# The whole tanh of a recurrence step, written to PSUM instead of SBUF

## The chip, the cores and the metric

One core of one Trainium2 chip runs the whole program in one launch. The metric is the device time in microseconds from the first to the last instruction's work, median of the runs shown.

## The reference

The input is x, 8 x 1024 x 256 in fp32. Four blocks are added one after another, each on a layer norm of x:

```python
x = x + attn_a(layernorm(x))      # gated linear attention, 16 heads, and an MLP 256 -> 512 -> 256
x = x + ffn(layernorm(x))         # 8 experts of 256 x 256, the top 2 of each token are mixed
x = x + attn_b(layernorm(x))      # a plain recurrence over the 1024 tokens
x = x + ffn(layernorm(x))
```

The change is in the third block. It is strictly serial in time, with a state of 16 numbers for each of the 8 batch rows:

```python
xB = einsum('bsd,dn->sbn', x, B)
def step(h, xb_t):
    h = tanh(xb_t + h @ A.T)
    return h, h
_, hs = scan(step, h0, xB)
y = einsum('sbn,nd->bsd', hs, C) @ W_out.T + b_out
```

## The kernel before

The 1024 tokens are cut into 32 rounds of TS = 32 tokens for all 8 batch rows (TOK = 256 columns, two tiles of 128 rows). A round goes through eight stages, and a software pipeline runs them skewed: in one body, stage 0 works on round n, stage 1 on round n-1, and so on to stage 7. Each engine has its own instruction list for the body, in an order written out by hand, and semaphores tie the lists together. So every engine runs its queue strictly in order, and an instruction that waits holds all behind it.

The recurrence of a round has 32 steps, spread between the other work of the bodies of stages 4 to 7. One step crosses three engines:

- TensorE, `step` and `recur` (L1113): waits for semaphore `rnn_h`, then one matmul of the constant aT with the 8 columns of hs of the step before adds to the 8 columns of this step in PSUM bank RB (bank 5, columns 0 to 255, which a matmul at L1397 has filled with x times B for all 32 steps). It signals `rnn_mm`.
- ScalarE, `state_of` (L525, L526): waits for `rnn_mm` and takes the tanh of these 8 columns twice, 48 partitions x 8: once rounded to fp32r (h_lead), once in full fp32 (h_whole). The second signals `rnn_tanh`.
- VectorE, `split_state` (L750): waits for `rnn_tanh`. One scalar_tensor_tensor multiplies h_whole by a 0/1 number per partition (`keeps_rest`, from the constants in SBUF) and subtracts h_lead, which gives the exact value split into two fp32r parts in hs. It signals `rnn_h`, for which TensorE's next step waits.

The split into parts is how fp32 accuracy is kept with fp32r matmuls; the helper `product` (L1096) does the same for all wide products, with three matmuls for each. `combine` (L781) is VectorE's scalar_tensor_tensor that adds one expert's output from PSUM, scaled per row by `coef`, to an accumulator in SBUF. `normed` on VectorE (L771) subtracts and multiplies two scalars per row. GpSimd has 128x256 and 128x512 tensor_tensors on SBUF: the expert sums (L396, L398), the attention state (L412, L422), residuals (L415, L425, L487), and small statistics (`rstd`, L368). Bank 5 is used for the recurrence alone, and its columns 256 to 511 are free.

Of the kernel before, what the change touches and what calls it, by code (L numbers as in the profile page):

```python
# [6 lines left out]
F32 = mybir.dt.float32  # L7
F32R = mybir.dt.float32r
U32 = mybir.dt.uint32
ALU = mybir.AluOpType  # L10
ACT = mybir.ActivationFunctionType
# [3 lines left out]
B, T, D = 8, 1024, 256  # L15
TS = 32
ROUNDS = T // TS
TOK = B * TS
# [13 lines left out]
NB = 3 * N  # L32
# [14 lines left out]

BANK = {"Y0": 3, "Z": 2, "QK": 6, "VG0": 2, "VG1": 0, "KT": 6, "SD": 0, "O": 4, "OG": 7, "WO": 7, "Y1": 6, "F1A": 3,
    "F1B": 6, "F2": 6, "T1": 2, "L1": 1, "G1_0": 7, "G1_1": 2, "G1_2": 3, "G1_3": 1, "G1_4": 7, "G1_5": 6, "G1_6": 0,
    "G1_7": 7, "TR": 3, "RB": 5, "RO": 4, "T2": 0, "L2": 0, "G2_0": 2, "G2_1": 1, "G2_2": 7, "G2_3": 3, "G2_4": 2, "G2_5": 1,  # L50
    "G2_6": 0, "G2_7": 6}
# [3 lines left out]
    0: [("T2", 6, 'yT2'), ("L2", 6, 'sub2'), ("G1_6", 4, ("acc1", 2 * VECTOR_GROUPS, 10)), ("VG1", 1, 'sg1'),  # L55
            ("G2_6", 6, ("acc2", 2 * VECTOR_GROUPS, 10)), ("SD", 1, 'dstate')],
    1: [("L1", 4, 'sub1'), ("G1_3", 4, ("acc1", 2 * VECTOR_GROUPS, 6)), ("G2_1", 6, ("acc2", 2 * VECTOR_GROUPS, 2)),
            ("G2_5", 6, ("acc2", 2 * VECTOR_GROUPS, 8)), ("SD", 1, 'dstate')],
    2: [("T1", 4, 'yT1'), ("G1_1", 4, ("acc1", 2 * VECTOR_GROUPS, 2)), ("Z", 1, 'zb'), ("G2_0", 6, ("scaled2", TILES, 1)),
            ("G2_4", 6, ("scaled2", TILES, 2)), ("VG0", 1, 'sg0'), ("SD", 1, 'dstate')],  # L60
    3: [("Y0", 1, 'hT'), ("G1_2", 4, ("acc1", 2 * VECTOR_GROUPS, 4)), ("F1A", 3, 'gT'),
            ("G2_3", 6, ("acc2", 2 * VECTOR_GROUPS, 6)), ("TR", 4, 'yrT'), ("SD", 1, 'dstate')],
    4: [("O", 2, 'onorm'), ("RO", 5, 'mv_m2')],
# [31 lines left out]
def build(nc, x, wts, out):  # L95
    ctx = ExitStack()
    with ctx:
        def sb(name, shape, dt=F32):
            return ctx.enter_context(nc.sbuf_tensor(name, shape, dt))
# [3 lines left out]
        def sem(name):  # L103
            if name not in sems:
                sems[name] = ctx.enter_context(nc.semaphore(name))
            return sems[name]
# [10 lines left out]
        keeps_rest, lead_sign, whole_sign = (cst[0:NB, C_PART + n:C_PART + n + 1] for n in range(3))  # L117
# [85 lines left out]
        yr, yrT = staged([TILES, D]), staged([KC, TOK])  # L203
        x2b = staged([TILES, D])
        hs = sb("hs", [P, B, TS], F32R)
        h_whole, h_lead = sb("h_whole", [NB, B]), sb("h_lead", [NB, B], F32R)


        ps = ctx.enter_context(nc.psum_tensor("ps", [P, 8, 512], F32))
        SD = BANK["SD"]  # L210

        def by_chunk(use):
            return ps[:, BANK[use], :].rearrange("p (c t) -> p c t", c=KC)
# [61 lines left out]
        def past(count):  # L275

            return max(count, 0) if isinstance(count, int) else count

        def value(eng, count):


            return past(count) if isinstance(count, int) else eng.to_reg(count)
# [210 lines left out]
        def _(act):  # L493
            a = nc.scalar
# [27 lines left out]
            def state_of(k, count):  # L522

                act.wait_ge(sem("rnn_mm"), past((count - 1) * TS + k + 1))
                a.activation(h_lead[:], ps[0:NB, BANK["RB"], k * B:(k + 1) * B], ACT.Tanh)  # L525
                a.activation(h_whole[:], ps[0:NB, BANK["RB"], k * B:(k + 1) * B], ACT.Tanh).then_inc(sem("rnn_tanh"), 1)  # L526

            def normed(dst, src, r):

# [29 lines left out]
            def body(it):  # L559
                c0, c1, c2, c3, c4, c5, c6, c7 = (cnt(it, k) for k in range(STAGES))  # L560
                if live(it, 7):
                    state_of(28, c7)
# [3 lines left out]
                if live(it, 7):  # L566
                    state_of(29, c7)
                    state_of(30, c7)
# [142 lines left out]
        def _(dve):  # L711
            v = nc.vector
# [30 lines left out]
            def split_state(k, count):  # L743

                target = value(dve, (count - 1) * TS + k + 1)
                if k == 0:
                    dve.wait_ge(sem("RO"), past(count - 1))
                dve.wait_ge(sem("pads_zero"), 1)
                dve.wait_ge(sem("rnn_tanh"), target)
                v.scalar_tensor_tensor(hs[0:NB, :, k], h_whole[:], keeps_rest, h_lead[:].bitcast(F32), ALU.mult, ALU.subtract).then_inc(sem("rnn_h"), 1)  # L750

            def split_experts(c):
                cols = slice(c * E * D, (c + 1) * E * D)
# [81 lines left out]
            def body(it):  # L835
# [5 lines left out]
                if live(it, 6):  # L841
                    split_state(29, c6)
# [8 lines left out]
                if live(it, 6):  # L851
                    split_state(30, c6)
# [4 lines left out]
                if live(it, 6):  # L857
                    split_state(31, c6)
# [45 lines left out]
                if live(it, 2):  # L904
                    dve.wait_ge(sem("DS1"), c2)
                    v.tensor_tensor(att[:], ps[:, SD:SD + J, 0:TOK].rearrange("p j (b t) -> p j b t", t=TS),
                                         causal.unsqueeze(1).unsqueeze(1).broadcast_to([P, J, B, TS]), ALU.mult).then_inc(sem("att"), 1)
# [594 lines left out]
```

## Time and profile before

| what | value |
|---|---|
| median of 3 runs | 2058.72 us (2046.99 to 2063.43) |
| profiled execution | 2060.23 us, span 2058.3 us |
| TensorE busy, of the span | 87% |
| VectorE busy | 77% |
| GpSimd busy | 55% |
| ScalarE busy | 46% |
| mean granted TensorE clock | 0.921 |

Busy is the time in which at least one instruction of the engine runs. TensorE's instructions overlap, so its busy share is not its share of peak. Its instruction list appears twice, PE for matmuls and PEld for weight loads; DVE is VectorE, ACT is ScalarE, POOL is GpSimd. The chain that ended last is found by going back from the last instruction to what released each one, so its shares tell on whom the end depended.

### The profile page before, as it was taken

What the parts mean: (1) busy time and instruction counts of PE and PEld (TensorE: products, weight loads), DVE (VectorE), ACT (ScalarE), POOL (GpSimd) and SP (SyncE); (2) the same over time, 40 slices, a digit from 0 to 9 for tenths busy, and PEclk for the clock granted to TensorE, in tenths of its full rate; (3) what the DMA queues carried; (4) which work ended last, traced back from release to release, by engine and by line L of the source; (5) the groups of instructions that cost most, each with busy time, mean ns of one, the idle gap of its engine ahead of it and who ended that gap; (6) DMA issues with size and microseconds to landing.
All of it is one profiled execution on the core that took longest, in us unless ns stands there. A gap on an engine that the chain in (4) does not pass through costs nothing.

```text
span 2058.3 us, 49764 instructions
## 1 busy us (share of the span) xinstructions
PE 1788.0 (87%) x15176; PEld 1482.2 (72%) x15176; DVE 1587.9 (77%) x4909; ACT 956.7 (46%) x3532; POOL 1130.2 (55%) x1451
## 2 busy tenths in 40 slices
PE   4687899899888999989899898989989898988876
PEld 3576777777777777777777777777777777777654
DVE  4676788778888878888877887887888788876554
ACT  4344544445554444555445455544544554444321
POOL 4765566566556556565655665555565556554211
PEclk8787999999999999999999999999999999998888
DMA  4100000000000000000000000000000000000000
GB/s 128 35 27 16 12 27 27 26 25 15 20 15 25 25 25 24 15 20 17 25 25 25 23 18 18 18 25 25 25 25 13 18 20 26 21 22 6 6 6 11
DMA packets 73360, 47.89 MB, mean 23 GB/s; under 512 B 39088, under 2 KB 72528, under 8 KB 73168
## 3 DMA queue, kind: packets, MB, share of 16 engines
q1 hardware_dynamic: 71648, 45.35, 7.4%
q10 hardware_dynamic: 1648, 1.72, 0.3%
q8 instruction: 35, 0.57, 0.1%
q14 instruction: 29, 0.24, 0.0%
HBM read 30.28 MB, written 16.78 MB: 23 GB/s over the span
## 4 chain that ended last, share of the span: by engine, by line
PE 65%; DVE 20%; issue 8%; ACT 4%; DMA 1%; SPq 1%; DVEq 0%; POOL 0%; ACTq 0%; POOLq 0%
PE ps L1096 51%; DVE hs L750 8%; PE ps L1113 5%; DVE y L771 4%; PE ps L1141 3%; ACT h_whole L526 2%; PE ps L1397 1%; DVE oh L824 1%; PE ps L1150 1%; PE ps L1129 1%; PE ps L1131 1%; ACT h_lead L525 1%; DVE stage L781 1%; DVE st_f L760 1%; DVE yT L833 1%
## 5 line engine op out<-in xcount | busy, mean ns | idle before, releaser
L1096 PE MATMUL ps<-we,yT 128*128 128x512 f32 x3072 | 907.3, 441 | 1.3 <-DVE mv L766 1.3
L1096 PEld LDWEIGHTS ps<-we,yT 128*128 128x128 f32 x3072 | 597.0, 208 | 116.0 <-DVE mv L766 1.5
L750 DVE SCALAR_TENSOR_TENSOR hs<-h_whole,cst,h_lead 48x8 fp32r<-48x8 f32 x1024 | 364.3, 356 | 322.8 <-ACT h_whole L526 322.0
L525 ACT ACTIVATE h_lead<-ps 48x8 fp32r<-48x8 f32 x1024 | 173.7, 170 | 855.6 <-PE ps L1113 850.9
L1113 PEld LDWEIGHTS ps<-hs,aT 128*128 128x128 f32 x1024 | 207.1, 202 | 261.7 <-issue 236.5
L1113 PE MATMUL ps<-hs,aT 128*128 128x8 f32 x1024 | 224.0, 219 | 145.0 <-DVE hs L750 139.2
L396 POOL TENSOR_TENSOR part<-part 128x256 f32<-128x256 f32 x64 | 52.0, 812 | 448.0 <-ACT part L544 448.0
L781 DVE SCALAR_TENSOR_TENSOR acc<-ps,coef,acc 128x256 f32<-128x256 f32 x384 | 184.9, 482 | 11.9 <-POOL acc L398 1.8
L781 DVE SCALAR_TENSOR_TENSOR stage<-ps,coef,stage 128x256 f32<-128x256 f32 x384 | 183.4, 478 | 11.9 <-POOL stage L398 4.5
L435 POOL TENSOR_TENSOR orstd<-omean,mhalf 128x32 f32<-128x32 f32 x32 | 176.2, 5505 | 2.7
L467 POOL TENSOR_TENSOR sx<-osq,cst 32x512 f32<-32x512 f32 x128 | 168.9, 1319 | 7.6
L526 ACT ACTIVATE h_whole<-ps 48x8 f32<-48x8 f32 x1024 | 161.4, 158 | 0.0
L396 POOL TENSOR_TENSOR stage<-stage 128x256 f32<-128x256 f32 x64 | 47.3, 739 | 193.7 <-ACT stage L544 193.7
L1096 PE MATMUL ps<-wa,gTs 128*128 128x256 f32 x768 | 108.1, 291 | 0.3 <-DVE gTs L833 0.3
L1096 PE MATMUL ps<-wa,hTs 128*128 128x512 f32 x384 | 108.2, 418 | 0.0
L1096 PE MATMUL ps<-h2Ts,wa 128*128 128x256 f32 x768 | 103.5, 285 | 0.0
L1102 PE MATMUL ps<-cst,y 128*128 128x128 f32 x256 | 45.3, 304 | 64.0 <-DVE y L771 64.0
L1096 PEld LDWEIGHTS ps<-h2Ts,wa 128*128 128x128 f32 x768 | 97.5, 191 | 4.1
L1096 PEld LDWEIGHTS ps<-wa,gTs 128*128 128x128 f32 x768 | 96.7, 194 | 0.4 <-issue 0.4
L771 DVE TENSOR_SCALAR y<-xmid,mv_f,rf 128x256 f32<-128x256 f32 x64 | 82.6, 1328 | 0.6 <-POOL rf L368 0.6
L1102 PEld LDWEIGHTS ps<-cst,y 128*128 128x128 f32 x256 | 29.8, 152 | 72.0 <-DVE y L771 46.7
L1096 PEld LDWEIGHTS ps<-wa,hTs 128*128 128x128 f32 x384 | 69.7, 195 | 14.2
(178 smaller groups left out, 3580.3 us busy)
## 6 DMA issues: line engine op xcount, KB each, us to landing
xin<-in_x SPq DMA_DIRECT2D x64, 128.0 KB
vrow<-vtok SPq DMA_DIRECT2D x32, 256.0 KB, 2.1
vx<-vrow SPq DMA_DIRECT2D x128, 64.0 KB, 2.0
xag<-in_x SPq DMA_DIRECT2D x64, 128.0 KB
out<-stage SPq DMA_DIRECT2D x64, 128.0 KB
stage<-in_experts SPq DMA_DIRECT2D x1, 2048.0 KB, 7.9
stage<-in_Wvg SPq DMA_DIRECT2D x1, 512.0 KB, 5.5
stage<-in_W SPq DMA_DIRECT2D x1, 512.0 KB, 4.5
```

The lines of the kernel that those rows point to most:

```text
L396: g.tensor_tensor(m.part[:, i, 0, :], m.part[:, i, 0, :], m.part[:, i, 1, :], ALU.add).then_inc(sem(f"part{m.s}"), 1)
L435: g.tensor_tensor(orstd[:], omean[:], mhalf[:], ALU.pow).then_inc(sem("orstd"), 1)
L467: g.tensor_tensor(sx[r, :, j * HQ * DV:(j + 1) * HQ * DV], smid[r], blockmask[r].unsqueeze(1).broadcast_to([32, B, HQ * DV]), ALU.mult).th ...
L525: a.activation(h_lead[:], ps[0:NB, BANK["RB"], k * B:(k + 1) * B], ACT.Tanh)
L526: a.activation(h_whole[:], ps[0:NB, BANK["RB"], k * B:(k + 1) * B], ACT.Tanh).then_inc(sem("rnn_tanh"), 1)
L750: v.scalar_tensor_tensor(hs[0:NB, :, k], h_whole[:], keeps_rest, h_lead[:].bitcast(F32), ALU.mult, ALU.subtract).then_inc(sem("rnn_h"), 1)
L771: ins = v.tensor_scalar(dst[:, i, :], src[:, i, :], mean[:, i:i + 1], scale[:, i:i + 1], ALU.subtract, ALU.mult)
L781: v.scalar_tensor_tensor(m.acc[:, i, :], ps[:, bank, e % 2 * D:(e % 2 + 1) * D], m.coef[:, i, e:e + 1], m.acc[:, i, :], ALU.mult, ALU.add) ...
L1096: ins = t.matmul(dst, left(lp, c), right(rp, c), start=(n == 1), stop=(n == 3 * chunks))
L1102: ins = t.transpose(ps[:, dst_bank, c * TOK + i * P:c * TOK + (i + 1) * P], src[:, i, c * P:(c + 1) * P], ident)
L1113: return t.matmul(ps[0:NP, BANK["RB"], k * B:(k + 1) * B], aT[:], hs[:, :, (k - 1) % TS], start=False, stop=True, skip_group_check=True)
L1141: ins = t.matmul(ps[:, SD + j, b * TS:(b + 1) * TS], kx[r, b, :, :].rearrange("p h t -> p (h t)"), qt[r, b * TS:(b + 1) * TS], start=True, ...
```

## The change

The tile h_whole leaves SBUF. It becomes columns 256 to 263 of PSUM bank 5, partitions 0 to 47, next to the columns from which the tanh is taken. The writer (L526) and the reader (L750) are otherwise the same, and so are all waits and signals.

```diff
-        h_whole, h_lead = sb("h_whole", [NB, B]), sb("h_lead", [NB, B], F32R)
+        h_lead = sb("h_lead", [NB, B], F32R)
 
 
         ps = ctx.enter_context(nc.psum_tensor("ps", [P, 8, 512], F32))
         SD = BANK["SD"]
+        h_whole = ps[0:NB, BANK["RB"], TOK:TOK + B]
@@
-                a.activation(h_whole[:], ps[0:NB, BANK["RB"], k * B:(k + 1) * B], ACT.Tanh).then_inc(sem("rnn_tanh"), 1)
+                a.activation(h_whole, ps[0:NB, BANK["RB"], k * B:(k + 1) * B], ACT.Tanh).then_inc(sem("rnn_tanh"), 1)
@@
-                v.scalar_tensor_tensor(hs[0:NB, :, k], h_whole[:], keeps_rest, h_lead[:].bitcast(F32), ALU.mult, ALU.subtract).then_inc(sem("rnn_h"), 1)
+                v.scalar_tensor_tensor(hs[0:NB, :, k], h_whole, keeps_rest, h_lead[:].bitcast(F32), ALU.mult, ALU.subtract).then_inc(sem("rnn_h"), 1)
```

## Rows read from the trace of the kernel before

**Rows 1.** The page: the chain that ended last, shares of the span by line

```profile
PE ps L1096 51%; DVE hs L750 8%; PE ps L1113 5%; DVE y L771 4%; PE ps L1141 3%; ACT h_whole L526 2%; PE ps L1397 1%; DVE oh L824 1%; PE ps L1150 1%; PE ps L1129 1%; PE ps L1131 1%; ACT h_lead L525 1%; DVE stage L781 1%; DVE st_f L760 1%; DVE yT L833 1%
```

**Rows 2.** Waits: who waited for whom, us in total, times, longest us

```profile
PE ps L1113 <- DVE hs L750: 139.2, 266, 1.8
...
PE ps L1102 <- DVE y L771: 64.0, 33, 7.2
```

**Rows 3.** The page's costliest groups: busy us, mean ns | idle before, who ended it

```profile
L750 DVE SCALAR_TENSOR_TENSOR hs<-h_whole,cst,h_lead 48x8 fp32r<-48x8 f32 x1024 | 364.3, 356 | 322.8 <-ACT h_whole L526 322.0
...
L526 ACT ACTIVATE h_whole<-ps 48x8 f32<-48x8 f32 x1024 | 161.4, 158 | 0.0
```

**Rows 4.** Single lines L750, L781: duration ns min/median/max, first and last start us

```profile
L750 DVE SCALAR_TENSOR_TENSOR hs<-h_whole,cst,h_lead x1024: 191/225/1266, 140.4 to 2028.0; 48x8 fp32r<-48x8 f32 x171
...
L781 DVE SCALAR_TENSOR_TENSOR acc<-ps,coef,acc x384: 466/484/487, 122.0 to 1972.9; 128x256 f32<-128x256 f32 x192
```

**Rows 5.** Timeline, 1011 to 1013 us: start us, us, instruction [idle before <-releaser]

```profile
1011.02 1.26 POOL L422 TENSOR_TENSOR state<-state,dstate 128x512 f32<-128x512 f32 x1
1011.05 1.26 DVE L750 SCALAR_TENSOR_TENSOR hs<-h_whole,cst,h_lead 48x8 fp32r<-48x8 f32 x1 [0.17 <-ACT h_whole L526]
...
1012.46 0.24 PE L1113 MATMUL ps<-hs,aT 128*128 128x8 f32 x1 [0.87 <-DVE hs L750]
```

**Rows 6.** Timeline, 1053 to 1058 us

```profile
1053.69 1.27 POOL L487 TENSOR_TENSOR res<-xag,b 128x512 f32<-128x512 f32 x1
...
1054.19 0.80 DVE L750 SCALAR_TENSOR_TENSOR hs<-h_whole,cst,h_lead 48x8 fp32r<-48x8 f32 x1
1054.91 2.67 DVE L771 TENSOR_SCALAR y<-xmid,mv_f,rf 128x256 f32<-128x256 f32 x2
1054.92 1.11 POOL L412 TENSOR_TENSOR state<-state,dec 128x512 f32<-128x512 f32 x1
...
1055.13 0.24 PE L1113 MATMUL ps<-hs,aT 128*128 128x8 f32 x1 [0.55 <-DVE hs L750]
...
1055.99 1.45 POOL L415 TENSOR_TENSOR stage<-acc,bout 128x512 f32<-128x512 f32 x1
```

**Rows 7.** Timeline, same round: a VectorE step, and recurrence matmuls that stood idle

```profile
1025.24 0.63 DVE L750 SCALAR_TENSOR_TENSOR hs<-h_whole,cst,h_lead 48x8 fp32r<-48x8 f32 x1
...
1026.01 0.24 PE L1113 MATMUL ps<-hs,aT 128*128 128x8 f32 x1 [0.62 <-DVE hs L750]
...
1042.67 0.24 PE L1113 MATMUL ps<-hs,aT 128*128 128x8 f32 x1 [0.33 <-DVE hs L750]
...
1045.38 0.24 PE L1113 MATMUL ps<-hs,aT 128*128 128x8 f32 x1 [0.15 <-DVE hs L750]
```

**Rows 8.** Groups by line and shape: small instructions on PSUM and on SBUF

```profile
L789 DVE TENSOR_TENSOR lg<-half,ps 128x16 f32<-128x16 f32 x64 | 10.9, 171 | 2.2
...
L802 DVE TENSOR_TENSOR sub<-lg,mx 128x16 f32<-128x16 f32 x64 | 10.0, 157 | 0.0
...
L557 ACT ACTIVATE emid<-gcum 128x8 f32<-128x8 f32 x32 | 6.6, 207 | 0.0
```

**Rows 9.** Timeline: once a round. Windows: length, busy PE PEld DVE ACT POOL, granted clock

```profile
981.21 1.02 PE L1397 MATMUL ps<-stage,bin_ 128*128 128x256 f32 x4
...
1040.07 1.02 PE L1397 MATMUL ps<-stage,bin_ 128*128 128x256 f32 x4
...
1101.84 1.02 PE L1397 MATMUL ps<-stage,bin_ 128*128 128x256 f32 x4
...
1162.22 1.02 PE L1397 MATMUL ps<-stage,bin_ 128*128 128x256 f32 x4
...
1004.20:1011.00 6.80, 6.29 (x65) 4.53 (x64) 5.31 (x21) 3.59 (x14) 1.58 (x2) 0.98 0.00 0
...
1065.70:1072.50 6.80, 5.74 (x65) 4.15 (x63) 6.06 (x21) 3.25 (x13) 2.81 (x3) 0.98 0.00 0
...
1072.50:1075.90 3.40, 3.17 (x9) 2.62 (x10) 2.29 (x14) 0.24 (x3) 1.28 (x2) 0.54 0.00 0
```

## The prediction

> **What bounds the kernel now.** I read the page's busy shares first, then its chain, then the waits, then one round of the timeline. TensorE is busy 87% of the span and VectorE 77% (the table above); half of the chain that ended last is the product helper L1096, and the next line in it is VectorE's recurrence instruction L750 with 8% [rows 1]. So TensorE sets the pace, with holes in it. The waits tell whose holes these are: TensorE's recurrence matmul waited 139.2 us in 266 places for L750, and its transposes 64.0 us in 33 places for the normalised tile of L771 [rows 2].
>
> Then the oddity on which everything here rests. L750 works on 48x8 elements. Its median is 225 ns and its mean 356 ns, with a longest of 1266 ns [rows 3, 4]: most of the 1024 are short and some are up to five times as long, for the same shape. (356 - 225) x 1024 = 134 us of VectorE's busy time is in those long ones. The timeline shows what they are. At 1011.05 us one takes 1.26 us and ends at 1012.31; GpSimd's L422, two SBUF inputs, runs from 1011.02 to 1012.28 [rows 5]. At 1054.19 one takes 0.80 and ends at 1054.99, while GpSimd's L487 ends at 1054.96 [rows 6]. Both start inside a GpSimd instruction and end 0.03 us after it. L750 isn't working there, it stands until GpSimd lets go of something that both need.
>
> **Which operand is it?** L750 reads two tensors, h_whole and h_lead, both in SBUF. The combine L781 is the same operation with the same kind of operands (a tensor, a scalar per partition from SBUF, a tensor), except that its first tensor is in PSUM. There are 768 of it, in two groups of 384, all over the span, while GpSimd is busy 55% of it; the group shown has median 484 and maximum 487 ns [rows 4], and the other is like it. Not one was held up. With h_whole in PSUM, L750 has L781's form. So I expect L750 at its short duration in all 1024 places.
>
> **The change part by part.** No instruction, wait or DMA is added or taken out; two operands move.
> (a) The hold-up goes. What it is worth is not the 134 us but the part that TensorE waits out. In the round from 1000 to 1061 us the recurrence matmuls that stood idle behind a long L750 are these:
> - 1012.46, idle 0.87; L750 before it is longer by 1.26 - 0.22 = 1.04, so all 0.87 goes [rows 5];
> - 1026.01, idle 0.62; L750 took 0.63, so 0.63 - 0.22 = 0.41 goes [rows 7];
> - 1036.98 (not shown) and 1042.67, 0.33 each, behind L750s of 0.72 and 0.55: 0.66 goes [rows 7];
> - 1045.38, 0.15, behind one of 0.45: 0.15 goes [rows 7];
> - 1055.13, idle 0.55 [rows 6]. This one I don't count, since TensorE then waits for L771's tile, which is done at 1057.58; see (b).
>
> Other long ones (at 1009.58, 1013.14, 1029.73, 1043.35) lie under matmuls that were still running, and are worth next to nothing. Sum 0.87 + 0.41 + 0.66 + 0.15 = 2.09 us a round. The neighbouring rounds repeat these waits. Of 32 rounds I count 29, because in the first and last few GpSimd has less to collide with: 2.09 x 29 = 61 us.
> What keeps it: after each of these waits TensorE runs back to back (from 1012.46 to about 1024 with no idle time), so it is the bound there and starts earlier by the whole amount.
> (b) The stretch at 1054 to 1058. L750 gets the slot that opens when L487 ends at 1054.96; the two instructions of L771, which are held up too, then stand behind L412 and L415 (2.67 us for two, which makes the last end at 1057.58) [rows 6]. With L750 out of the queue the first L771 can take the slot at 1054.96, and the second the one behind L412, which starts some 0.4 us later for it: L412 then ends at 1054.96 + 0.4 + 1.11 = 1056.5, and the second ends some 0.3 later, at 1056.75. Gain 0.83 if the slots fall so, 0 if GpSimd's next instruction wins each of them. I take 0.5: 0.5 x 29 = 15 us.
> (c) The granted clock. Rounds last, by one matmul that runs once in each, 58.86 us (981.21 to 1040.07), then 61.77, then 60.38, and so on in turn [rows 9]. The work is the same. The long one has a stretch at 1072.50 to 1075.90 with a granted clock of 0.54, about the lower level (1.2 of 2.4 GHz); before it TensorE was busy 5.74 of 6.80 us. One round earlier it was busy 6.29 of 6.80 in that place, at 0.98, and no such stretch follows [rows 9]. The idle 0.87 of (a) lies in this place of every round, so after the change TensorE idles less there than in either of the two rounds. Price of such a stretch: 61.77 - 60.38 = 1.39 us; one round in three has it: 1.39 x 10 = 14 us. If the other half-clock stretch of each round shrinks too, all rounds go to 58.86: the mean of the three, 60.34, less that is 1.5, x 29 = 43 us. I keep 14.
> (d) The prices of PSUM. VectorE: a tensor_tensor on 16 elements takes 171 ns with one input in PSUM (L789) and 157 ns with both in SBUF (L802), so +14 ns [rows 8]. The other bound is no difference. I take 14. Some eleven L750s a round release TensorE directly: 0.014 x 11 x 29 = 4 us. ScalarE writes PSUM nowhere in this trace. Nearest is the read side: 8 elements SBUF to SBUF take 207 ns (L557), PSUM to SBUF 158 (L526) [rows 3, 8], so PSUM costs it up to 49 ns less for a read. For the write I bound by +49 and -49 ns, the same 319 steps: 16 us either way. I take 0.
> The Trainium skill, page Perfetto Trace Analysis, section Optimizing Scalar/DVE Operations, speaks against half of this: some 60 ns of overhead for VectorE on SBUF and 125 on PSUM, and the reverse for ScalarE, 93 on SBUF and 51 on PSUM. As an estimate by that page, each step would cost 65 - 42 = 23 ns more, 7 us in all in place of my 4. This trace shows 14 where the page has 65.
> (e) What is late next. VectorE gets 4 us a round back, so its queue is not the next bound; GpSimd's instructions come a little earlier against VectorE's, and other instructions with two SBUF inputs (the scan L1022, kx L855, the rests of L833) may fall on them. These meet GpSimd rarely or under running matmuls now. I put 1 us in every fifth round on it, 6 us, as a guess.
>
> Sum: -61 - 15 - 14 + 4 + 6 = -80 us; with the small recoveries left out of (a), some 0.1 us a round, -83. The profiled execution took 2060.23 us (span 2058.3) and the median of the runs is 2058.72, so they are one number for this purpose: 2058.7 - 83 = 1975 us.
>
> **Rivals.**
> - *Freed but given back.* TensorE arrives earlier at waits for someone else: L771's tile, ScalarE's wide instructions, a bank that the combines still hold. For it: the 0.55 at 1055.13 is such a case already, and the mean wait on L771 is 2 us [rows 2]. Against: four of the five places are followed by uninterrupted matmuls. If two thirds are lost: 61/3 = 20, no (b) or (c), +10 of (d) and (e): about 2048. In between, half lost, 2020.
> - *The clock gives more.* All half-clock stretches beyond the shortest round's go, and (b) is whole: 61 + 24 + 43 = 128, about 1930. For it: the three lengths of a round. Against: the deepest hole (1050 to 1058) is shortened only a little.
> - *The hold-up stays.* If h_lead and the scalar keep L750 on what GpSimd uses, nothing moves but (d): 2063. Against it L781, 768 times, with an SBUF scalar too.
> - *Slower.* ScalarE writes the bank (5) from which it reads in the same instruction, and VectorE reads it, and each access pays a stall. It decides from 83/319 = 0.26 us a step; a step stalled 0.35 us gives 2058.7 - 83 + 112 = 2088. For it: no row shows ScalarE writing PSUM. Against: TensorE writes no column of that bank while the two are at it, since its next step waits for L750, and 0.26 us is more than either whole instruction's difference between any two memories in the rows.
>
> **How the numbers follow.** Forecast as summed, 1945 to 2005: 0.70. More by the clock, down to 1930 and a little under: 0.10. Partly or mostly given back, 2005 to 2050: 0.14, half of it under 2020. Hold-up stays: 0.03. Slower: 0.03. Range 1930 to 2018. A measurement of this kernel can tell about 1%, 20 us: faster than 2038 holds 0.70 + 0.10 + 0.12 = 0.92, within 1% 0.05, slower 0.03.
>
> **What the profile after would show.** L750's maximum under 300 ns and its mean at 225 to 245; VectorE busy some 120 to 130 us less; TensorE's wait for L750 down from 139 to about 60 to 75 us; the 0.87 us hole gone and with it the second half-clock stretch in most rounds; rounds of 57 to 58 us; L771's pair shorter than 2.67 us; L526 between 110 and 200 ns. The prediction is wrong if L750 still has durations over 500 ns, if L526 or L750 grow by more than 0.1 us, or if TensorE's waits for L750 go down while those for L771, ScalarE or the banks go up by as much.

## The result: twice the forecast gain

| | before | after |
|---|---|---|
| median of the runs | 2059.81 us (4 runs) | 1884.22 us (4 runs, 1874.65 to 1886.15) |
| ratio | | 0.9148, 95% interval 0.9098 to 0.9199 |
| span of the profiled execution | 2058.3 us | 1881.6 us |
| mean granted TensorE clock | 0.921 | 0.940 |

The forecast was 1975 us, range 1930 to 2018. The kernel became 176 us faster where 84 were forecast. The sign and the mechanism were right, and the size was half. All lines of the code after the edit at the tile's declaration stand one number higher in the changed kernel (L750 is L751, L771 is L772, L1113 is L1114). In the experiments, lines behind an added one stand up to three numbers higher than in the kernel before.

First the page of the changed kernel: busy us (share of the span), and the chain by line, which answer to the table of before and to [rows 1].

```profile
PE 1716.5 (91%) x15176; PEld 1443.7 (77%) x15176; DVE 1437.7 (76%) x4909; ACT 960.5 (51%) x3532; POOL 1131.3 (60%) x1451
...
PE ps L1097 55%; PE ps L1114 4%; PE ps L1142 3%; DVE hs L751 3%; PE ps L1103 2%; DVE y L772 2%; PE ps L1130 2%; PE ps L1132 2%; PE ps L1398 2%; DVE oh L825 1%; PE ps L1151 1%; DVE stage L782 1%; DVE yT L834 1%; DVE st_f L761 1%; ACT ps L527 1%
```

VectorE's recurrence instruction fell from 8% of the chain to 3%, and L771 from 4% to 2%. VectorE is busy 150 us less for the same instructions. Next the single line L751 of the changed kernel (duration ns min/median/max), two of its waits, and the costliest-group rows of the ScalarE write and of L772, which answer to [rows 2 to 4]; the last row is L771's group in the kernel before:

```profile
L751 DVE SCALAR_TENSOR_TENSOR hs<-ps,cst,h_lead x1024: 190/222/228, 140.3 to 1851.3; 48x8 fp32r<-48x8 f32 x171
...
PE ps L1114 <- DVE hs L751: 62.8, 130, 2.1
...
PE ps L1103 <- DVE y L772: 41.0, 30, 7.2
...
L527 ACT ACTIVATE ps<-ps 48x8 f32<-48x8 f32 x1024 | 162.3, 158 | 0.0
...
L772 DVE TENSOR_SCALAR y<-xmid,mv_f,rf 128x256 f32<-128x256 f32 x64 | 62.2, 1011 | 0.6 <-POOL rf L369 0.6
...
L771 DVE TENSOR_SCALAR y<-xmid,mv_f,rf 128x256 f32<-128x256 f32 x64 | 82.6, 1328 | 0.6 <-POOL rf L368 0.6
```

The longest of 1024 is now 228 ns where it was 1266, the median 222 where it was 225. ScalarE's write to PSUM takes the same 158 ns as the one to SBUF. So the move itself shows no price in the durations on either engine, and every hold-up of this instruction is gone. The two of L771 took 1328 ns each in the kernel before, and 1011 now: still held up, but less.

The timeline of the changed kernel in the stretch of [rows 6], where L750 stood 0.80 us, the pair of L771 took 2.67, and TensorE waited:

```profile
1021.33 1.27 POOL L488 TENSOR_TENSOR res<-xag,b 128x512 f32<-128x512 f32 x1
...
1021.82 0.22 DVE L751 SCALAR_TENSOR_TENSOR hs<-ps,cst,h_lead 48x8 fp32r<-48x8 f32 x1
1021.95 1.84 DVE L772 TENSOR_SCALAR y<-xmid,mv_f,rf 128x256 f32<-128x256 f32 x2
...
1022.18 0.24 PE L1114 MATMUL ps<-hs,aT 128*128 128x8 f32 x1
...
1022.56 1.09 POOL L413 TENSOR_TENSOR state<-state,dec 128x512 f32<-128x512 f32 x1
...
1023.61 1.32 POOL L416 TENSOR_TENSOR stage<-acc,bout 128x512 f32<-128x512 f32 x1
...
1023.85 0.66 PE L1103 MATMUL ps<-cst,y 128*128 128x128 f32 x4 [0.89 <-DVE y L772]
```

GpSimd runs the same three instructions. VectorE's L751 passes beneath the first of them (1021.33 to 1022.60) in 0.22 us, and the pair ends 1.97 us after the start of L751, where it was 3.39 us before (1054.19 to 1057.58).

### The profile page after: what moved, and what is told of

Same layout as the page of the kernel before. It is cut to its first block, busy times and chain, and to the rows that moved or that the text cites. A ratio compares the mean times of both kernels' runs of the same rounds, so it can differ in the third digit from the quotient of the medians.

```text
span 1881.6 us, 49764 instructions
## 1 busy us (share of the span) xinstructions
PE 1716.5 (91%) x15176; PEld 1443.7 (77%) x15176; DVE 1437.7 (76%) x4909; ACT 960.5 (51%) x3532; POOL 1131.3 (60%) x1451
## 4 chain that ended last, share of the span: by engine, by line
PE 72%; DVE 14%; issue 8%; ACT 3%; DMA 1%; SPq 1%; POOL 0%; DVEq 0%; ACTq 0%; POOLq 0%
PE ps L1097 55%; PE ps L1114 4%; PE ps L1142 3%; DVE hs L751 3%; PE ps L1103 2%; DVE y L772 2%; PE ps L1130 2%; PE ps L1132 2%; PE ps L1398 2%; DVE oh L825 1%; PE ps L1151 1%; DVE stage L782 1%; DVE yT L834 1%; DVE st_f L761 1%; ACT ps L527 1%
## 5 line engine op out<-in xcount | busy, mean ns | idle before, releaser
L1097 PE MATMUL ps<-we,yT 128*128 128x512 f32 x3072 | 863.9, 425 | 1.3 <-DVE mv L767 1.3
L1097 PEld LDWEIGHTS ps<-we,yT 128*128 128x128 f32 x3072 | 569.1, 199 | 109.2 <-DVE mv L767 1.5
L526 ACT ACTIVATE h_lead<-ps 48x8 fp32r<-48x8 f32 x1024 | 174.5, 170 | 677.2 <-PE ps L1114 670.4
L751 DVE SCALAR_TENSOR_TENSOR hs<-ps,cst,h_lead 48x8 fp32r<-48x8 f32 x1024 | 224.1, 219 | 292.7 <-ACT ps L527 290.5
L1114 PEld LDWEIGHTS ps<-hs,aT 128*128 128x128 f32 x1024 | 200.8, 196 | 155.6 <-issue 120.1
L1114 PE MATMUL ps<-hs,aT 128*128 128x8 f32 x1024 | 218.8, 214 | 64.8 <-DVE hs L751 62.8
L527 ACT ACTIVATE ps<-ps 48x8 f32<-48x8 f32 x1024 | 162.3, 158 | 0.0
L1142 PE MATMUL ps<-qt,kx 32*128 32x32 f32 x2048 | 65.2, 276 | 1.8
```

The source lines that it names most:

```text
L527: a.activation(h_whole, ps[0:NB, BANK["RB"], k * B:(k + 1) * B], ACT.Tanh).then_inc(sem("rnn_tanh"), 1)
L751: v.scalar_tensor_tensor(hs[0:NB, :, k], h_whole, keeps_rest, h_lead[:].bitcast(F32), ALU.mult, ALU.subtract).then_inc(sem("rnn_h"), 1)
L1097: ins = t.matmul(dst, left(lp, c), right(rp, c), start=(n == 1), stop=(n == 3 * chunks))
L1114: return t.matmul(ps[0:NP, BANK["RB"], k * B:(k + 1) * B], aT[:], hs[:, :, (k - 1) % TS], start=False, stop=True, skip_group_check=True)
L1142: ins = t.matmul(ps[:, SD + j, b * TS:(b + 1) * TS], kx[r, b, :, :].rearrange("p h t -> p (h t)"), qt[r, b * TS:(b + 1) * TS], start=True, ...
```

## Where the time went, step by step

TensorE's matmul of each recurrence step comes 32 times a round, so the interval from one to the next tells where a round became shorter. The table is worked out from the timelines: medians of ns over the rounds in the middle of the run; "hs" is the duration of the VectorE instruction of the step in the first column. Some rounds have a stretch in which TensorE is granted half its clock, 3.4 us or a multiple of it. For before, the rounds of 58.8 us are taken, and for after those of 54.4 us: both have one such stretch, so they compare at equal clock. For e10 the rounds of 57.3 us are taken, which have none; every other round there has one and lasts 58.8 us. The rounds of e14 alternate between some 55.3 and 56.8 us, and its last entry lies between. Steps 10 and 11 stand here for the clock. Intervals not shown differ by less than 0.05 us, except step 9 in e8, where a half-clock stretch makes it 1.68 us instead of 1.01.

```
          interval from step k to k+1              hs of step k
  k     before  five   step+7  filled  after  +wait    before  step+7  after
                (e8)   (e14)   (e10)          (e9)             (e14)
  0      1373   1049    1048    1373    1048   1048      549     224     224
  2      1146    912     912    1142     912    913      459     225     225
  7      2071   2073    1488    2068    1482   1480      799     216     216
  8      3339   3337    2916    3365    2499   1379      214     631     211
  10     2609   2919    2852    1589    2530   1592      225     226     223
  11     2052   2600    2490    1504    2134   1502      225     226     223
  14     1830   1829    1828    1828    1580   1567      706     705     219
  15     2019   1011    1011    2019     935    936     1259     223     223
  22     2283   1856    1856    2283    1853   1856      626     197     196
  26     1555   1551    1552    1550    1500   1500      220     220     224
  27     1757   1766    1765    1762    1648   1650      217     217     218
  29     1444    936     936    1428     936    936      733     224     224
  round 58821  57936   56018   57254   54452  51780
```

Two things are to be seen. Where the hold-up was what TensorE waited for, the interval shrinks by the whole difference in L750's duration: step 15 by 1.08 us (1.01 in e8), step 29 by 0.51, step 7 by 0.59. And the interval after step 8, in which L750 itself was never long before, shrinks by 0.84. Together 4.4 us a round at equal clock, against the 2.6 that the prediction had for (a) and (b).

## Experiments

**Which of the two, the write or the read?** Three kernels. The first puts the other operand into PSUM:

```diff
-        h_whole, h_lead = sb("h_whole", [NB, B]), sb("h_lead", [NB, B], F32R)
+        h_whole = sb("h_whole", [NB, B])
+        h_lead = ps[0:NB, BANK["RB"], TOK:TOK + B]
...      # its writer and its reader follow
```

> The mirror image: h_lead goes to the free columns of bank 5, h_whole stays in SBUF. ScalarE's last write of a step, the one that signals, is to SBUF as in the kernel before. Theory P (port: a VectorE instruction with two SBUF tensor inputs stands until GpSimd's instruction ends): again one SBUF tensor, so the recurrence instruction's maximum is under 300 ns, mean 215 to 230, and the time that of the changed kernel, 1884 us within 10. Theory W (ScalarE's signalling write is quicker to PSUM, or lands where VectorE finds it sooner): nothing gained, about 2059, durations up to 1266 ns as before.

Measured 1878.01 us, ratio 0.9145 (0.9113 to 0.9177).

The second keeps the change's write and undoes its read. VectorE reads a tile that was set to zero at the start, so the exact tanh is left out, and the order of work stays:

```diff
-                v.scalar_tensor_tensor(hs[0:NB, :, k], h_whole, keeps_rest, ...
+                v.scalar_tensor_tensor(hs[0:NB, :, k], h_zero[:], keeps_rest, ...   # h_zero: SBUF
```

> ScalarE writes h_whole to PSUM as in the changed kernel, but VectorE reads in its place a tile of zeros in SBUF (this leaves the exact tanh out of the recurrence, the order of work is the same). Theory P: two SBUF tensors again, mean 340 to 370 ns, maximum over 1200 ns, time 2059 within 15. Theory W: 1884 within 10.

Measured 2053.24 us, ratio 1.0002 (0.9984 to 1.0020).

The third does the reverse on the kernel before, with the zeros in the free columns of bank 5:

```diff
-                v.scalar_tensor_tensor(hs[0:NB, :, k], h_whole[:], keeps_rest, ...
+                v.scalar_tensor_tensor(hs[0:NB, :, k], h_zero, keeps_rest, ...      # h_zero: PSUM
```

> The other half: ScalarE writes h_whole to SBUF as before, VectorE reads in its place zeros from the free columns of bank 5 (the exact tanh is left out in the same way). Theory P: maximum under 300 ns, time 1884 within 10. Theory W: 2059. If both halves give something, the two gains add up to 175 us.

Measured 1881.06 us, ratio 0.9173 (0.9137 to 0.9209). The recurrence instruction in the three, in this order (duration ns min/median/max):

```profile
L751 DVE SCALAR_TENSOR_TENSOR hs<-h_whole,cst,ps x1024: 186/219/226, 133.8 to 1847.2; 48x8 fp32r<-48x8 f32 x171
```

```profile
L752 DVE SCALAR_TENSOR_TENSOR hs<-h_zero,cst,h_lead x1024: 191/225/1266, 137.8 to 2019.1; 48x8 fp32r<-48x8 f32 x171
```

```profile
L752 DVE SCALAR_TENSOR_TENSOR hs<-ps,cst,h_lead x1024: 190/222/229, 134.3 to 1840.0; 48x8 fp32r<-48x8 f32 x171
```

The read does everything and the write nothing, and it doesn't matter which of the two tensors is in PSUM. Theory W is out.

**Is it GpSimd?** In the trace of the kernel before, 298 of the 1024 L750s took more than 300 ns, and each of them ends 0.02 to 0.04 us after one of GpSimd's wide tensor_tensors. So both kernels were run with the wide ones cut to 8 or 16 columns, which leaves out most of what they compute. One of these edits, as an example:

```diff
-                g.tensor_tensor(m.part[:, i, 0, :], m.part[:, i, 0, :], m.part[:, i, 1, :], ALU.add)
+                g.tensor_tensor(m.part[:, i, 0, 0:8], m.part[:, i, 0, 0:8], m.part[:, i, 1, 0:8], ALU.add)
```

> The kernel before (h_whole in SBUF), with GpSimd's ten wide elementwise instructions cut to 8 to 16 columns each (most of the expert sums, attention state, residuals and gate are left out; every instruction, wait and order stays). Their hold of 0.7 to 1.3 us each shrinks to some 0.2. Theory P: the recurrence instruction has nothing long to stand behind, its mean falls to 225 to 250 ns and its maximum to under 500, and the time falls to that of the changed kernel or below, since L771's two are freed as well: 1880 down to 1830. Theory W: GpSimd's length matters only by its own waits, which the chain doesn't show: 2059 within 20.

> The changed kernel with the same cut of GpSimd's instructions (the same parts left out). Theory P: nearly equal to the run before it, at most 20 us less (short GpSimd instructions can still hold an SBUF-SBUF one for 0.2 us), not 175 us less; against the changed kernel it shows what L771's hold-up still costs, some 30 us. Theory W: 175 us less than the run before it.

Measured 1792.50 us (ratio 0.8717, 0.8678 to 0.8756) and 1792.08 us (0.8704, 0.8672 to 0.8737). First the kernel before so cut, then the changed one: its recurrence instruction, and L771's group (busy us, mean ns).

```profile
L752 DVE SCALAR_TENSOR_TENSOR hs<-h_whole,cst,h_lead x1024: 192/224/259, 128.3 to 1760.6; 48x8 fp32r<-48x8 f32 x171
...
L773 DVE TENSOR_SCALAR y<-xmid,mv_f,rf 128x256 f32<-128x256 f32 x64 | 23.2, 401 | 0.6 <-POOL rf L370 0.6
```

```profile
L753 DVE SCALAR_TENSOR_TENSOR hs<-ps,cst,h_lead x1024: 190/222/228, 129.8 to 1761.6; 48x8 fp32r<-48x8 f32 x171
```

With GpSimd's wide tensor_tensors cut short the change is worth 0.4 us, which is within the noise. So the whole effect of the change is the hold-up by them. The 92 us between 1884 and 1792 are what GpSimd's length still costs the changed kernel, and L771 at 401 ns in place of 1011 names the first suspect.

**How much does each place carry?** Four kernels that use PSUM at some steps only, chosen as the program is built:

```diff
+        IN_PSUM = (7,)          # (15,)   (0, 2, 15, 22, 29)   (0, 2, 7, 15, 22, 29)
+        h_psum = ps[0:NB, BANK["RB"], TOK:TOK + B]
-                v.scalar_tensor_tensor(hs[0:NB, :, k], h_whole[:], keeps_rest, ...
+                v.scalar_tensor_tensor(hs[0:NB, :, k], h_psum if k in IN_PSUM else h_whole[:], keeps_rest, ...
```

(the same choice in ScalarE's write).

> h_whole in PSUM for step 7 of each round alone, SBUF for the other 31 (the choice is made when the program is built). This is the step that stood 0.80 us at 1054.19 and whose 0.55 us of TensorE idle time I did not count, since TensorE waits for the normalised tile of L771 next. As the prediction put it: 0 to 0.83 us a round, at most 24 us in all. By the step-by-step table of both traces (step 7 earlier by 0.59, and the next interval shorter by 0.84 besides): 1.43 us x 31 = 44 us, and up to 1.5 us more in rounds where a half-clock stretch goes. So 2059 - 24 = 2035 or more against 2059 - 44 = 2015 or less.

Measured 1993.95 us, 60 less than before, ratio 0.9716 (0.9681 to 0.9752). The step that the forecast valued at 0 to 24 us brings 60. By the timelines about half of that is time freed at equal clock, 1.0 us a round: step 7's interval is 0.59 us shorter, and step 8's only 0.42, since step 8's own L750 takes 631 ns here. The other half is the clock, whose mean is 0.936 where it was 0.921.

> h_whole in PSUM for step 15 of each round alone. The prediction counted the 0.87 us of TensorE's idle row: 0.87 x 29 = 25 us, and 14 for the half-clock stretch behind it. By the difference in L750's own duration, which TensorE's start follows one for one: 1.08 x 31 = 34 us, plus the stretch in up to every third round, 14 us. So 2054 - 25 - 14 = 2015 against 2054 - 34 - 14 = 2006; without the clock's part 2029 against 2020.

Measured 1984.24 us, 74 less, ratio 0.9660 (0.9615 to 0.9706): more than either expectation. Only 1.01 us a round of it, 31 us, is step 15's interval.

> h_whole in PSUM for steps 0, 2, 15, 22 and 29 of each round: the five places that the prediction counted, and no other. As the prediction put it: 61 us and 14 for the clock, 2054 - 75 = 1979. By the step table of the two traces: 0.32 + 0.23 + 1.08 + 0.43 + 0.50 = 2.57 us x 31 = 80 us, and 14 to 44 for the clock: 1960 to 1930. If the other places (7, 14, 26, 27) carry what is missing, this kernel and the one with step 7 alone add up to 2054 - 1884 less about 0.4 x 31 = 13 us.

Measured 1982.12 us, 76 less, ratio 0.9640 (0.9602 to 0.9678). This looked like the forecast's 1979 come true, and it isn't. Five places give no more than step 15 alone, though the table shows each of the five shorter by its full amount (column e8), 2.5 us a round or 77 us. The difference is the clock. The profiled executions say so: the mean granted clock is 0.933 with step 15 alone and 0.923 with the five, beside 0.921 before. With two levels, 1 and 1/2, a mean of c over a span means 2 x (1 - c) x span at the lower one: 325 us before, 304 with the five, 265 with step 15 alone, 226 in the changed kernel. And their place counts as well. With step 15 alone, 12 of 21 middle rounds have one of their stretches on steps 5 and 6, and it costs nothing there: the steps 5 to 8 take 8.5 us, as in the rounds without it. With the five, only two rounds have one there, and the others have theirs on steps 9 to 11.

**What the clock is worth by itself.** TensorE gets work to do in the hole before L771's tile, which is this row of the kernel before, and nothing is released sooner:

```profile
1057.64 0.66 PE L1102 MATMUL ps<-cst,y 128*128 128x128 f32 x4 [1.75 <-DVE y L771]
```


```diff
+                    if live(it, 5):
+                        for _ in range(6):
+                            t.matmul(ps[:, BANK["Y1"], :], wa[:, 0, 0:P], wa[:, 0, 0:512], start=True, stop=True)
                     pe.wait_ge(sem("y1"), c3)
                     transposed(BANK["Y1"], y1).then_inc(sem("Y1"), 1)
```

> The kernel before, with six 128x512 matmuls added in each round where TensorE stands for L771's tile (idle 1.75 us), into the bank that the transposes overwrite next. Nothing that waits is released sooner. Theory C (part of the gain is the granted clock: holes are followed by half-clock stretches, 1.5 us each): half-clock time falls from 329 us and the time with it, by 14 to 45 us, 2054 to 2010. Rival: the clock follows something else, or the added work costs what it saves: 2054 to 2080.

Measured 1992.92 us, ratio 0.9678 (0.9660 to 0.9697): 66 us less than before, by six useless matmuls a round. The windows of one such stretch, first before, then filled (length; busy of PE, PEld, DVE, ACT, POOL with counts; granted clock; DMA share and GB/s):

```profile
1050.00:1058.80 8.80, 6.05 (x69) 4.40 (x70) 7.97 (x15) 4.56 (x16) 5.79 (x9) 1.00 0.15 46
1058.80:1065.70 6.90, 6.90 (x27) 5.61 (x28) 2.28 (x14) 2.25 (x10) 0.00 (x0) 0.52 0.16 55
```

```profile
1016.70:1025.50 8.80, 7.44 (x76) 5.43 (x76) 8.00 (x15) 4.62 (x17) 5.74 (x8) 1.00 0.16 47
```

In this round of the kernel before, some 6.9 us at half clock follow the hole; in the filled kernel half of the rounds have none. The table's column e10 has the intervals of steps 10 and 11 at 1.59 and 1.50 us, their length at full clock, where before they are 2.61 and 2.05. That is 1.57 us for a stretch of 3.4 us, and many rounds of the kernel before have two or three such stretches.

> The changed kernel with four such matmuls in the same place (idle 0.89 us there). Theory C: most of the 3.4 us at half clock per round go, 1884 - 45 = 1839; with part of them 1860. Rival: 1884 to 1900.

Measured 1848.57 us, ratio 0.8962 (0.8928 to 0.8996), 36 us less than the changed kernel: all but the early and late rounds run without a half-clock stretch, at 52.9 us.

**Does the forecast's sum hold at equal clock?** The five steps with the six matmuls:

> h_whole in PSUM at steps 0, 2, 15, 22, 29 and the six added matmuls ahead of TensorE's wait for L771's tile. Theory A (the freed time adds at equal clock; the five steps alone gave 76 us because nearly each round still had 6.8 us at half clock): the kernel with the matmuls alone, 1993, less 2.5 us x 31 = 77, so 1916 within 12. Theory B (the five places give back part of what they free to other waits): 1940 or more.

Measured 1896.54 us, ratio 0.9249 (0.9210 to 0.9288), 96 us less than with the matmuls alone (92 if each is set against the kernel before as measured alongside it). Theory B is out: nothing was given back. It is even 15 to 20 us more than the 77 of theory A. The timelines show why: the remaining half-clock stretch falls on steps 5 and 6 in most rounds, ahead of the wait for L771's tile, where TensorE would wait anyway. Step 5's interval is 2.59 us in place of 1.80 and step 6's 1.62 in place of 1.34, but step 7's is 1.02 in place of 2.07. Half of that last gain is a hold-up that the delay avoids: step 7's L750 now comes just before the end of GpSimd's L489 (L487 of the kernel before) and takes 0.22 us, although both of its tensors are in SBUF:

```profile
525.61 1.28 POOL L489 TENSOR_TENSOR res<-xag,b 128x512 f32<-128x512 f32 x1
```

```profile
526.78 0.22 DVE L752 SCALAR_TENSOR_TENSOR hs<-h_whole,cst,h_lead 48x8 fp32r<-48x8 f32 x1
```

So the same stretch costs nothing in this kernel's steps 5 and 6, and 1.57 us on steps 10 and 11. It is not the place alone: in the changed kernel, where step 7 is free already, three of 21 middle rounds have the stretch on steps 5 and 6, and the steps 5 to 8 take 8.34 us there in place of 7.13.

> h_whole in PSUM at the five steps and at step 7. By the step table the places left out (1, 14, 16, 25 and what follows from them at 26 and 27) are worth 0.25 + 0.06 + 0.11 = 0.4 us a round: 1884 + 13 = 1897, and up to 1.5 us a round more if they decide on a half-clock stretch. If step 7 brings only what it brings alone by its own row (0.59 of 1.43 us): 1884 + 13 + 26 = 1923.

Measured 1918.02 us, ratio 0.9332 (0.9284 to 0.9380). That is neither 1897 nor quite 1923. The table has the reason in the row of step 8: its L750 takes 631 ns here, where it took 214 in the kernel before and 211 in the changed one. With step 7 freed, everything behind it is earlier, and step 8 now runs into GpSimd's third wide instruction. The timeline of this kernel (L417 and L752 are L415 and L750 of the kernel before):

```profile
1046.14 1.32 POOL L417 TENSOR_TENSOR stage<-acc,bout 128x512 f32<-128x512 f32 x1
```

```profile
1046.85 0.64 DVE L752 SCALAR_TENSOR_TENSOR hs<-h_whole,cst,h_lead 48x8 fp32r<-48x8 f32 x1
```

It ends at 1047.49, GpSimd's at 1047.46. The hold-ups of before were not all that the form could suffer; this one, 0.42 us a round, was waiting behind another. The kernel with step 7 alone in PSUM has it too, with the same 631 ns. The changed kernel is rid of it since it has all 32 steps in PSUM.

**A version that is faster than both.** L771 is still held up by the three wide instructions that GpSimd starts right after it has computed L771's scale. In the changed kernel GpSimd is idle for some 9.5 us right behind them, so it may wait:

```diff
                     pool.wait_ge(sem("x1"), past(c3 - 1))
+                    pool.wait_ge(sem("y1"), c3)
                     g.tensor_tensor(res[:], xag[:], b2[:].unsqueeze(1).broadcast_to([P, TILES, D]), ALU.add).then_inc(sem("res"), 1)
```

> The changed kernel, and GpSimd waits for the semaphore of L771's tile (y1) before its first wide residual add (L487 of the kernel before), so that none of the three wide instructions behind it can hold L771's two up. GpSimd is idle for some 10 us after them, so that costs it nothing. Theory P: L771's pair on xmid falls from 1.84 us to about 0.75, TensorE's transposes of it start some 1.0 us earlier in each round, 1884 - 31 = 1853, and 1.5 us more in each round in which the half-clock stretch goes (down to 1810). If the pair is late for another reason (its statistics, the queue ahead): 1884 within 8.

Measured 1805.74 us, ratio 0.8763 (0.8742 to 0.8784): 78 us less than the changed kernel, and the fastest here with all of its work done. The pair, and GpSimd behind it:

```profile
980.78 0.72 DVE L773 TENSOR_SCALAR y<-xmid,mv_f,rf 128x256 f32<-128x256 f32 x2
...
981.58 1.28 POOL L489 TENSOR_TENSOR res<-xag,b 128x512 f32<-128x512 f32 x1 [2.04 <-DVE y L773]
```

The pair takes 0.72 us where it took 1.84; the interval after step 8 is 1.38 us (column e9), 1.12 less, or 35 us in 31 rounds; and with the hole most rounds lose their last half-clock stretch (clock 0.961, 141 us at half against 226), some 39 us more (85 us / 3.4 x 1.57).

> The changed kernel with both: GpSimd waits for y1, and four added matmuls ahead of TensorE's wait for y1. If the first takes the hole away, the four matmuls have nothing to hide under and cost their length, 4 x 0.21 = 0.85 us a round: 26 us more than with GpSimd's wait alone, less what the clock gives. Between 1815 and 1880; the two gains don't add.

Measured 1822.89 us, ratio 0.8855 (0.8838 to 0.8871): 17 us slower than with the wait alone. As expected the gains don't add; once the hole is gone the added matmuls are work like any other.

> The kernel before with the one wait of GpSimd for y1 ahead of L487, h_whole in SBUF as before. L487 then cannot hold step 7 up either, and L771's pair is free: by the step table of the runs 0.59 (step 7) + 3.34 - 1.38 = 1.96 (the interval after it), 2.55 us x 31 = 79 us, and up to 45 for the clock, less what the moved GpSimd instructions now hit at steps 8 to 10 (up to 1.3 us a round, 40 us): 1975 to 1935. If the hold-up isn't GpSimd's doing: 2055.

Measured 1951.47 us, ratio 0.9502 (0.9461 to 0.9542): one wait on GpSimd, without PSUM, is worth 103 us of the kernel before. Step 7's L750 is short there (215 ns), but GpSimd's instructions, which now come later, meet others: step 8's takes 846 ns and step 10's 467. With the tanh in PSUM the same wait has no such price.

## Why the prediction was half right

**Right.** The reading of L750's durations; the choice of L781 as precedent for the new form (maximum 228 ns against the 300 allowed); that no other engine becomes the bound; that the hold-up, not ScalarE's write, is what pays. The rival of a slower kernel, and that of a hold-up that stays, are out by the first profile. "Freed but given back" is out by the runs: the kernel with five steps and the added matmuls kept all 77 us and more, and from before to after no interval of the table grew by more than 0.05 us but those with a half-clock stretch.

**Wrong, by the terms of the sum**, in us a round:

| step of the prediction | forecast | measured |
|---|---|---|
| (a) the five places counted | 2.09 | 2.57 |
| (a) 1055.13 (step 7), not counted | 0 | 0.59 |
| (a) the long ones "under matmuls" (step 14; from 25 to 27) | 0.1 | 0.41 |
| (b) L771's stretch | 0.5 | 0.84 |
| (c) the clock | 14 us in all | some 45 us in all (99 us less at half clock / 3.4 x 1.57) |
| (d), (e) PSUM's price, new collisions | -10 us in all | none seen |
| rounds | 29 | 31 |

4.4 x 31 = 137, and 45 for the clock, make 182 where 176 were measured; the first and last rounds gain less than the middle ones.

- *(a) took the idle time as a ceiling.* The prediction capped each gain at the idle time printed beside TensorE's matmul: 0.87 at 1012.46 [rows 5], 0.33 at 1042.67, 0.15 at 1045.38 [rows 7]. That time counts from the modelled end of the pipelined matmul before, and is short of what TensorE can gain. The changed kernel's matmuls of steps 15 and 16:

```profile
1035.23 0.17 PE L1114 MATMUL ps<-hs,aT 128*128 128x8 f32 x1
1036.16 0.24 PE L1114 MATMUL ps<-hs,aT 128*128 128x8 f32 x1
```

  0.93 us from one to the other, and 2.02 before (1010.44 to 1012.46): 1.09 gained where the row had 0.87. The right measure was the releaser's own excess, 1.04, since TensorE started 0.15 us after it both times. By the same cap the place at 1009.58, whose matmul showed hardly any idle time, was called worth next to nothing and gave 0.25.
- *(a) and (b) had too little for step 7 and the pair behind it.* (a) put the idle time at 1055.13 at nothing, since TensorE waits for L771's tile next, and (b) took 0.5 of at most 0.83 for the tile. The runs have 0.59 + 0.84 = 1.43 us from the matmul of step 7 to that of step 9, which is what the tile gained. (b) did let the pair move up when L750 leaves the queue ahead of it; its working failed at L412. That one was to start 0.4 us later for the first of the pair, so that the pair would end 1.79 us after L487 (1056.75 against 1054.96) in place of 2.62. In the changed kernel it starts where GpSimd's first ends, at 1022.56, with no delay, and the pair ends 1.19 us after GpSimd's first (1023.79 against 1022.60). Step 7 alone was worth 60 us, half of it by the clock.
- *(c) had the clock at a third of its size.* Price and mechanism were right (1.39 us forecast, 1.57 measured for a stretch), the count was not. The prediction looked at one hole, step 15's, and took one stretch in three rounds away. The hole of 1050 to 1058, "shortened only a little" in the rival's words, lost 1.4 us, and the half-clock time went from about 6.8 us a round to 3.4, from 325 to 226 us in all. The rounds don't come "in turn" either, as the prediction read them: 58.8, 60.4 and 61.8 us follow each other in no fixed order, with one, two and three stretches of 3.4 us. The rival "The clock gives more" had the right reason and, with 43 us, nearly the measured size of this term; with (a) and (b) undersized its 1930 was still too slow.
- *(e) looked for new collisions in the wrong place.* It feared them for other instructions. The one that the runs found is L750's own at step 8, and the change protects against it.

On (d): the Trainium skill, page Perfetto Trace Analysis, section Optimizing Scalar/DVE Operations, has VectorE's overhead on PSUM some 65 ns above that on SBUF. The runs don't show it in the duration: the median is 222 ns with PSUM and 225 without.

What stays open: why the half-clock stretch sits where it does in a round. The runs show what it costs: 1.57 us on steps 10 and 11; on steps 5 and 6 nothing where step 7's hold-up follows, and 1.2 us in the changed kernel. That this decides some 20 us between kernels of the same freed time is shown, but not how one would plan for it.

## What to carry to other kernels

When an instruction of one fixed shape has a mean far above its median, look at which other engine's instruction its long ones end with. Here VectorE's instruction with two SBUF tensors beside wide GpSimd work was safe as soon as either tensor was in PSUM. Value such a release by the excess of the releasing instruction where the waiting engine follows it at a fixed distance, count everything behind it in its own queue as well, and don't cap it by the printed idle time. And price TensorE's holes twice, once as time and once as the clock that is lost behind them: filling a hole with useless matmuls is a quick experiment that measures the second part.

## What the runs showed of the hardware

- A VectorE instruction of 8 elements with two SBUF tensors stood up to 1266 ns behind GpSimd, and ended some 0.03 us after it; with one tensor in PSUM, whichever, none of 1024 was over 229 ns in the four kernels looked at above (after, e1, e3, e5). The Trainium skill, page SBUF — State Buffer, section Who interferes with whom, has the rule: VectorE's second SBUF input comes through a read port that it shares with GpSimd. These runs agree, but for the next point.
- Not all GpSimd instructions with two SBUF inputs hold it. The power of L435 takes 5.5 us, and L750 passes beneath it at its short duration, in the kernel before too. In its trace 60 of them lie wholly beneath one, at 215 to 230 ns. One such pair:

```profile
1017.40 5.50 POOL L435 TENSOR_TENSOR orstd<-omean,mhalf 128x32 f32<-128x32 f32 x1
```

```profile
1018.43 0.22 DVE L750 SCALAR_TENSOR_TENSOR hs<-h_whole,cst,h_lead 48x8 fp32r<-48x8 f32 x1
```

- VectorE's tensor_scalar on 128x256 fp32 from SBUF to SBUF (L771), with one tensor input only, is held in the same way: 401 ns each with GpSimd's wide instructions cut short, 1328 in the kernel before.
- ScalarE writing the PSUM bank that it reads, beside columns that a matmul has written, costs the same 158 ns as writing SBUF, and VectorE starts 0.10 us after its end in both.
- Six added matmuls a round made the kernel before 66 us faster.
